# Self attention of a decoder layer: a low score product over 128 rows, and one buffer of normalised outputs

## Chip, cores and metric

The kernel runs on one core of one Trainium2 chip. The metric is the device time of one execution in microseconds, as the median of several. The engines are named as in the profile: PE (TensorE matmuls) with PEld (its weight loads), DVE (VectorE), ACT (ScalarE), POOL (GpSimd) and SP (the DMA queue of SyncE).

## The reference, cut to what matters

One decoder layer over x of 8 batches x 512 tokens x 512 channels, in three blocks: a self attention, a cross attention with a router, and a feed-forward block over routed tokens. Only the first is touched. With h the normalised input, 16 heads of 64 and a causal window of 512 it computes

```
q, k, v = h @ w_q, h @ w_k, h @ w_v            # per head: [512, 64]
ll      = q @ k.T * 64**-0.5, causal
scores  = h @ scorer_w + scorer_b              # the 128 best tokens of the batch ...
attn    = softmax(concat(ll, lg))              # ... count a second time as keys
x       = x + (x' + (attn @ v) @ w_out)
```

A batch is one window of 512 tokens, so that the chosen 128 keys are keys of the window once more; the kernel gives them the weight two ("twice") instead of gathering them.

## The kernel before

`self_attention` runs a prologue (constants, weights split into a high and a low part, the first batch normalised) and then a loop over 8 batches. All four engines walk through one list of steps, `attention_plan()`, in the same order, each doing its part of a step; semaphores tie them together.

**Steps of one batch.** First the value projections (`v`) and the first `q` and `k`. Then 8 pairs of heads (p) with 5 score units each (u), 40 units in all, numbered g = 5p + u. At place g of the list PE does, in this order: the scores of unit g (`s`), the transposes of the probabilities of unit g-2 (`t`), the product with the values of unit g-3 (`pv`), at u = 0 the projection `q` and at u = 2 the projection `k` of the next pair, at four places something of the next batch (at g = 18 `score`, the transposes that make a row of the token scores), and last `ot`, the transposes of a finished pair's normalised outputs. The list puts `ot` of pair p at g = 5p + 9, a place with u = 4. After the pairs comes `out`, the product with w_out.

**A score unit.** u = 0 and u = 1 are one block of 128 queries by 512 keys (head 0 and 1). u = 2 and u = 3 are two blocks, of 128 and of 384 keys. u = 4 is two blocks of 256 keys, one of each head. Each block is three matmuls into `s_bank`: "high" (L661, or L659), 128 rows deep, whose stationary operand is `q_both` (a head's q rounded to fp32r in its own 64 rows and its remainder in the other 64) against `k_twice` (the rounded k in both halves); "low" (L664, or L657), 64 rows deep, the rounded q of the head's own rows against `k_lo`, the remainder of k; and the causal mask (L665), bf16. A pair so has 8 low products. At u = 4 the first block has its low product (L657) first, and PE waits (`s_half`) before the second block's.

**The other engines.** At place g DVE takes the row maxima of unit g (L525, L530), copies the transposed probabilities of unit g-2 to `probs_t` (L538, which the `pv` of that unit reads one place later), normalises the outputs of unit g-3 into `o_norm` (L552, L553), and at u = 3 makes `k_lo` of the next pair (L518), for which the scores of the next pair wait. The copy of the score row into `row_s` (L446) is at g = 18, behind `k_lo`. ACT takes the exponentials (L405), four half copies into `k_twice` at u = 3, and copies `ot` out (L413).

**Banks.** `t`, `score`, `ht` and `ot` take the two banks `pt_bank` in turn, in the order of the list; `PT` is that order. Before PE writes one (`pt_empty`) it waits until the use before the last one has been copied out; of a `score` that is the signal `row_copied` of L446.

`o_norm` has two buffers, one for each parity of the pair; DVE waits at u = 0 for the `ot` of the pair before the last.

Of the kernel before, what the change touches and what calls it, by code (L numbers as in the profile page):

```python
# [18 lines left out]
F32 = mybir.dt.float32  # L19
# [9 lines left out]
P = 128  # L29
# [55 lines left out]
def attention_plan():  # L85

    plan = [("v", i) for i in range(2 * TT - 2)] + [("q", 0), ("q_lo", 0), ("k", 0), ("k_lo", 0)]
    plan += [("v", i) for i in range(2 * TT - 2, 2 * TT)]
    for g in range(NU + 7):
        p, u = divmod(g, UNITS)
        if g < NU:
            plan.append(("s", g))
        if 2 <= g < NU + 2:
            plan.append(("t", g - 2))  # L100
        if 3 <= g < NU + 3:
            plan.append(("pv", g - 3))
        if g < NU and p + 1 < NPAIR and u < 4:
            plan.append((("q", "q_lo", "k", "k_lo")[u], p + 1))
        if g == 5:
            plan.append(("stats", 0))
        if g == 14:
            plan.append(("dot", 0))
        if g == 18:
            plan.append(("score", 0))  # L110
        if g in RANK_AT:
            plan.append(("rank", RANK_AT.index(g)))
        if NU <= g < NU + DC:
            plan.append(("ht", g - NU))
        if g >= 9 and (g - 9) % UNITS == 0 and (g - 9) // UNITS < NPAIR - 1:
            plan.append(("ot", (g - 9) // UNITS))
    plan.append(("ot", NPAIR - 1))
    plan += [("out", t) for t in range(TT)]
    return plan
# [7 lines left out]
def self_attention(nc, x, norm_w, w_q, w_k, w_v, w_out, scorer_w, scorer_b, x1):  # L127
# [3 lines left out]
    with ExitStack() as ctx:  # L131
        def sb(name, shape, dt=F32):
            return ctx.enter_context(nc.sbuf_tensor(name, shape, dt))
# [15 lines left out]
        q_both, k_twice = sb("q_both", [P, 2, 2, S], F32R), sb("k_twice", [P, 2, 2, S], F32R)  # L149
        k_lo = sb("k_lo", [P, 2, S], F32R)  # L150
        probs = sb("probs", [P, 2, 512])
        probs_t = sb("probs_t", [P, 2, 512])
        o_rden = sb("o_rden", [P, 2, 2])
        o_norm = sb("o_norm", [P, 2, TT, 2, HD])
        o_t = sb("o_t", [P, NPAIR, S])
# [4 lines left out]
        before = sb("before", [P, S + P * (TT - 1)], I8)  # L160
        row_s = sb("row_s", [P, S])
        junk = sb("junk", [P, S], BF16)
        carrier = sb("carrier", [P, 4])
# [28 lines left out]
        v_ready, v_sum_ready, qk_hi, qk_lo = sem("v_ready"), sem("v_sum_ready"), sem("qk_hi"), sem("qk_lo")  # L192
        s_ready, s_half = sem("s_ready"), sem("s_half")
        max_ready, p_ready = sem("max_ready"), sem("p_ready")
# [53 lines left out]
        def _(sp):  # L248
# [3 lines left out]
            sp.dma_start(sw[:, :], scorer_w.rearrange("d o -> o d").broadcast_to((P, D))).then_inc(small_in, 16)  # L252
            sp.dma_start(row_s[:, :], norm_w.rearrange("(o d) -> o d", o=1).broadcast_to((P, D))).then_inc(small_in, 16)
            sp.dma_start(sbias[:, :], scorer_b.rearrange("(o d) -> o d", o=1).broadcast_to((P, 1))
# [34 lines left out]
        def _(pl):  # L289
# [17 lines left out]
            nc.gpsimd.tensor_copy(ident_b[:, :], ident[:, :]).then_inc(const_made, 1)  # L307
            nc.gpsimd.memset(junk[:, :], 0.0).then_inc(const_made, 1)
            pl.wait_ge(const_made, N_CONST)
# [106 lines left out]
        def _(dv):  # L416
# [15 lines left out]

            def dot(n):

                dv.wait_ge(h_ready, n * TT + TT)
                for t in range(TT):
                    step(nc.vector.tensor_tensor_reduce(junk[:, :], xb[:, t, :], sw[:, :], 1.0, 0.0, ALU.mult,
                                                             ALU.add, score[:, t:t + 1]))
                done.wait(dv)
                nc.vector.tensor_scalar(score[:, :], score[:, :], sbias[:, 0:1], None, ALU.add).then_inc(score_ready, 1)  # L440

            def score_row(b, n):

                slot, ready = pt(b, ("score", 0))
                dv.wait_ge(pt_ready, ready)
                nc.vector.tensor_copy(row_s[:, :], pt_bank[slot][:, :]).then_inc(row_copied, 1)  # L446

            def rank(b, n, t):

                if t == 0:  # L450
                    dv.wait_ge(row_copied, n + 1)
                step(nc.vector.tensor_scalar(junk[:, :], row_s[:, :], score[:, t:t + 1], None, ALU.is_gt, ALU.add,
                                                  accum_out=cnt[:, 0, t:t + 1]))
                y0 = P * (TT - 1 - t)
                step(nc.vector.scalar_tensor_tensor(junk[:, :], row_s[:, :], score[:, t:t + 1],
                                                         before[:, y0:y0 + S], ALU.is_equal, ALU.mult,
                                                         accum_out=cnt[:, 1, t:t + 1]))
                if t == TT - 1:
                    done.wait(dv)
                    step(nc.vector.tensor_tensor(cnt[:, 0, :], cnt[:, 0, :], cnt[:, 1, :], ALU.add))  # L460
                    if b is not None:
                        dv.wait_ge(v_ready, n * (2 * TT))
                    nc.vector.tensor_scalar(twice[:, :], cnt[:, 0, :], TOPK - 0.5, 1.0, ALU.is_lt,
                                            ALU.add).then_inc(twice_ready, 1)
# [20 lines left out]
            dv.wait_ge(small_in, 64)  # L485
            nc.vector.tensor_tensor(sw[:, :], sw[:, :], row_s[:, :], ALU.mult).then_inc(sw_made, 1)
            dv.wait_ge(sw_made, 1)
            split(0)
            split(1)
            for c in range(DC):  # L490
                normed(None, 0, c)
            dot(0)
            split(2)
# [6 lines left out]
            with dv.Fori(0, B) as b, done.loop(b, 2 * TT + 2 * TT + 1 + NU, B):  # L500
                for kind, i in plan:
# [6 lines left out]
                    if kind in ("q_lo", "k_lo"):  # L508
                        slot, _ = pj(b, (kind[0], i))
                        dv.wait_ge(qk_hi, b * (2 * NPAIR) + 2 * i + (1 if kind == "q_lo" else 2))  # L510
                        for h in range(2):
# [5 lines left out]
                            else:  # L517
                                ins = nc.vector.tensor_tensor(k_lo[own, i % 2, :], pj_bank[slot][own, :],  # L518
                                                              k_twice[own, i % 2, h, :].bitcast(F32), ALU.subtract)
# [19 lines left out]
                    if kind == "pv":  # L539
                        p, u = divmod(i, UNITS)  # L540
                        dv.wait_ge(pv_ready, b * NU + i + 1)
                        if u == 0 and p >= 2:
                            dv.wait_ge(pt_ready, pt(b, ("ot", p - 2))[1])
                        n = len(unit_blocks(u))
                        src = o_bank[i % 2][:, 0:n * VW].rearrange("p (n v) -> p n v", n=n)
                        if u < 2:
                            dst = o_norm[:, p % 2, 3:4, u, :]
                        elif u < 4:
                            dst = o_norm[:, p % 2, 0:3:2, u - 2, :]
                        else:  # L550
                            dst = o_norm[:, p % 2, 1, :, :]
                        step(nc.vector.reciprocal(o_rden[:, i % 2, 0:n], src[:, :, HD]))  # L552
# [5 lines left out]
                    if kind == "dot":  # L558
                        dot(b + 1)
                    if kind == "score":  # L560
# [13 lines left out]
        def _(pe):  # L574
# [46 lines left out]
            with pe.Fori(0, B) as b:  # L621
                for kind, i in plan:
# [22 lines left out]
                    if kind == "s":  # L645
# [6 lines left out]
                        for h, t, c0, nk in unit_blocks(u):  # L652
                            queries, rows = slice(P * t, P * t + P), head_rows(h)
                            high = (q_both[:, p % 2, h, queries], k_twice[:, p % 2, h, 0:nk])
                            low = (q_both[rows, p % 2, h, queries], k_lo[rows, p % 2, 0:nk])
                            if u == UNITS - 1 and h == 0:
                                nc.tensor.matmul(s_bank[slot][:, c0:c0 + nk], *low, start=True, stop=False  # L657
                                                 ).then_inc(s_half, 1)
                                nc.tensor.matmul(s_bank[slot][:, c0:c0 + nk], *high, start=False, stop=False)  # L659
                            else:  # L660
                                nc.tensor.matmul(s_bank[slot][:, c0:c0 + nk], *high, start=True, stop=False)  # L661
                                if u == UNITS - 1:
                                    pe.wait_ge(s_half, b * NPAIR + p + 1)
                                nc.tensor.matmul(s_bank[slot][:, c0:c0 + nk], *low, start=False, stop=False)  # L664
                            ins = nc.tensor.matmul(s_bank[slot][:, c0 + nk - P:c0 + nk], ident_b[:, :], causal_b[:, :],  # L665
                                                   start=False, stop=True)
# [25 lines left out]
                    if kind == "ot":  # L692
# [3 lines left out]
                        for t in range(TT):  # L696
                            ins = nc.tensor.transpose(pt_bank[slot][:, P * t:P * t + P],
                                                      o_norm[:, i % 2, t, :, :].rearrange("p h d -> p (h d)"),
                                                      ident[:, :])
# [1062 lines left out]
```

## Time and profile before

| | us |
|---|---|
| median of 3 runs | 2416.09 (2413.26 to 2416.24) |
| span of the profiled execution, first to last instruction | 2414.0 |
| PE busy | 2241.6 (93%) |
| PEld busy | 1682.4 (70%) |
| DVE busy | 1349.6 (56%) |
| ACT busy | 845.5 (35%) |
| POOL busy | 429.2 (18%) |

The profiled execution's own time is its span, 2414.0 us; the median lies 2.1 us above it. The loop over the batches of the self attention lies between about 32 and 1648 us. Matmuls are pipelined and the ends that the profile gives for them are modelled, so that neighbouring matmuls seem to overlap: what a matmul costs is read from its start to the start of the next one. A time of a row has two decimals, so that a difference of two starts is good to 0.01 us.

### The profile page before, as it was taken

The page shows a single profiled execution, that of the slowest core. Times are in us where ns is not written, and L with a number is a line of the kernel's source. Part 1 is how long each engine was busy: PE and PEld are TensorE (multiplying, and loading weights), DVE is VectorE, ACT ScalarE, POOL GpSimd, SP SyncE. Part 2 cuts the span into 40 slices and gives each one's busy share as a digit, 9 for nine tenths or more (in the row PEclk, how much of TensorE's full clock was granted, in tenths as well). Part 3 has the DMA queues.
Part 4 walks back from the last instruction along what each step waited for, and adds up shares of the span by engine and source line. Part 5 has one row for each costly group of instructions (what it writes and reads, how often), then busy time and mean ns, then how long its engine had stood idle before and what let it go on. Part 6 is the DMA issues. An engine that isn't in the chain of part 4 may idle for free. (4 is left out here: it accounts for less than half of the span.)

```text
span 2414.0 us, 35686 instructions
## 1 busy us (share of the span) xinstructions
PE 2241.6 (93%) x12029; PEld 1682.4 (70%) x12029; DVE 1349.6 (56%) x3145; ACT 845.5 (35%) x1541; POOL 429.2 (18%) x669
## 2 busy tenths in 40 slices
PE   3999999999999999999999999996898888878899
PEld 3786777678678677767767767773787888865543
DVE  4574376177257437617725743661787878845500
ACT  3442344144144234314414423441644444413210
POOL 2100000010010000001001000002866666620000
PEclk9999999999999999999999999997988888858999
DMA  5000000100100000010010000002013211141000
GB/s 183 1 1 31 23 1 10 45 1 1 54 1 1 31 23 1 10 45 1 1 54 1 1 28 27 1 10 91 29 56 102 83 55 55 53 152 50 1 0 18
DMA packets 46136, 80.23 MB, mean 33 GB/s; under 512 B 10067, under 2 KB 10067, under 8 KB 45448
## 3 DMA queue, kind: packets, MB, share of 16 engines
q1 hardware_dynamic: 45320, 75.85, 9.3%
q8 instruction: 103, 1.69, 0.3%
q0 software_dynamic: 640, 2.10, 0.2%
q14 instruction: 73, 0.60, 0.1%
HBM read 60.11 MB, written 17.83 MB: 32 GB/s over the span
## 5 line engine op out<-in xcount | busy, mean ns | idle before, releaser
L405 ACT ACTIVATE probs<-s_bank,nmax 128x512 f32<-128x512 f32 (+3 forms) x512 | 249.4, 525 | 421.6 <-DVE nmax L530 294.3
L530 DVE TENSOR_REDUCE nmax<-s_bank 128x1 f32<-128x512 f32 (+2 forms) x384 | 185.3, 510 | 305.7 <-PE s_bank L665 302.0
L688 PE MATMUL o_bank<-vals,probs_t 128*128 128x65 f32 x2560 | 322.2, 269 | 0.0
L688 PEld LDWEIGHTS o_bank<-vals,probs_t 128*128 128x128 f32 x2560 | 311.0, 192 | 1.4 <-DVE probs_t L538 1.4
L712 PE MATMUL pj_bank<-w_o,o_t 128*128 128x512 f32 x512 | 223.5, 597 | 6.0 <-ACT o_t L413 6.0
L538 DVE COPY probs_t<-pt_bank 128x512 f32<-128x512 f32 x320 | 218.0, 681 | 3.6 <-PE pt_bank L673 3.6
L319 POOL TENSOR_TENSOR idle<-ones 128x4 f32<-128x4 f32 x41 | 8.1, 198 | 1065.7 <-DMA probs<-in_x 1063.7
L673 PE MATMUL pt_bank<-ident,probs 128*128 128x128 f32 x1280 | 194.1, 274 | 0.0
L712 PEld LDWEIGHTS pj_bank<-w_o,o_t 128*128 128x128 f32 x512 | 97.2, 191 | 127.6 <-issue 127.6
L664 PE MATMUL s_bank<-k_lo,q_both 64*128 64x512 f32 (+3 forms) x448 | 184.9, 413 | 0.0
L514 DVE SCALAR_TENSOR_TENSOR q_both<-pj_bank,q_both 64x512 fp32r<-64x512 f32 x128 | 88.2, 689 | 141.6 <-ACT q_both L392 138.9
L661 PE MATMUL s_bank<-k_twice,q_both 128*128 128x512 f32 (+3 forms) x448 | 166.9, 373 | 0.0
L383 ACT ACTIVATE vals<-pj_bank,twice 128x512 f32<-128x512 f32 x64 | 43.9, 688 | 341.8 <-PE pj_bank L579 336.5
L1259 PEld LDWEIGHTS x_o_bank<-vx,p_t 77*128 77x128 f32 x1024 | 148.9, 224 | 17.2 <-issue 10.0
L1259 PE MATMUL x_o_bank<-vx,p_t 77*128 77x33 f32 x1024 | 143.8, 300 | 3.9 <-DVE att L1141 3.9
L570 DVE TENSOR_TENSOR probs<-pj_bank,probs 128x512 f32<-128x512 f32 x32 | 22.1, 692 | 213.8 <-PE pj_bank L712 195.3
L664 PEld LDWEIGHTS s_bank<-k_lo,q_both 64*128 64x128 f32 x448 | 81.9, 183 | 85.5 <-issue 72.1
L673 PEld LDWEIGHTS pt_bank<-ident,probs 128*128 128x128 f32 x1280 | 135.7, 141 | 0.0
L577 PE MATMUL pj_bank<-wv_hi,ht_hi 128*128 128x512 f32 x256 | 104.2, 407 | 22.9 <-ACT vals L383 9.9
L1245 PE MATMUL e_bank<-qk_bd,xl_t 128*128 128x308 f32 x256 | 96.9, 510 | 27.7 <-DVE e L1123 27.0
L1022 POOL TENSOR_TENSOR e<-e,fill 128x616 f32<-128x616 f32 x64 | 95.3, 1489 | 127.1 <-DVE fill L1129 126.9
L665 PE MATMUL s_bank<-causal_b,ident_b 128*128 128x128 bf16 x512 | 117.7, 230 | 0.0
(266 smaller groups left out, 4245.5 us busy)
## 6 DMA issues: line engine op xcount, KB each, us to landing
xb<-in_x SPq DMA_DIRECT2D x9, 1024.0 KB, 5.3
xt<-x SPq DMA_DIRECT2D x36, 256.0 KB, 2.8
probs<-in_x SPq DMA_DIRECT2D x32, 256.0 KB, 2.7
x<-probs SPq DMA_DIRECT2D x32, 256.0 KB, 2.0
am<-in_L_ffn_attention_mask SPq DMA_DIRECT2D x8, 1024.0 KB, 5.2
out<-x SPq DMA_DIRECT2D x32, 256.0 KB, 2.1
w_sb<-in_L_ffn_w SPq DMA_DIRECT2D x2, 4096.0 KB, 20.2
o_t<-in_L_attn_w_v SPq DMA_DIRECT2D x2, 1024.0 KB, 9.5
```

The costliest lines, as they stand in the source:

```text
L405: ins = nc.scalar.activation(probs[:, i % 2, c0:c0 + nk], s_bank[i % 2][:, c0:c0 + nk], ACT.Exp, bias=nmax[:, i % 4, n:n + 1])
L530: ins = nc.vector.tensor_reduce(nmax[:, i % 4, n:n + 1], s_bank[i % 2][:, c0:c0 + nk], AX.X, ALU.max, negate=True)
L538: nc.vector.tensor_copy(probs_t[:, i % 2, :], pt_bank[slot][:, :]).then_inc(ts_ready, 1)
L577: nc.tensor.matmul(out, lhs_hi, rhs_hi, start=start, stop=False)
L661: nc.tensor.matmul(s_bank[slot][:, c0:c0 + nk], *high, start=True, stop=False)
L664: nc.tensor.matmul(s_bank[slot][:, c0:c0 + nk], *low, start=False, stop=False)
L665: ins = nc.tensor.matmul(s_bank[slot][:, c0 + nk - P:c0 + nk], ident_b[:, :], causal_b[:, :], start=False, stop=True)
L673: ins = nc.tensor.transpose(pt_bank[slot][:, P * j:P * j + P], probs[:, i % 2, P * j:P * j + P], ident[:, :])
L688: ins = nc.tensor.matmul(o_bank[slot][:, o0:o0 + VW], probs_t[:, i % 2, c0 + P * kt:c0 + P * kt + P], vals[:, kt, 2 * p + h, :], start=(kt ...
L712: ins = nc.tensor.matmul(pj_bank[slot][:, :], o_t[:, c, P * i:P * i + P], w_o[:, c, :], start=(c == 0), stop=(c == NPAIR - 1))
L1245: ins = nc.tensor.matmul(e_bank[:, c, 0:CH * SK], xl_t[:, (i // 2) % 2, P * k:P * k + P], qk_bd[:, n.par, k].rearrange("p h k -> p (h k)") ...
L1259: ins = nc.tensor.matmul(o_bank[:, VX * h:VX * h + VX], p_t[:, i % 2, h // CH, P * (h % CH):P * (h % CH) + P], vx[:, n.par, 2 * CH * (i % ...
```

## The change

- `k_lo` has a buffer for each head, 128 rows deep, in which the other head's 64 rows are zero. The low product is now 128 rows deep, with the same stationary operand as the high one. POOL clears all of `k_lo` once in the prologue, in place of the former memset of `junk`, before the signal for which DVE and PE start.
- At u = 4 the order is high, low, mask as in the other units, and the wait on `s_half` is gone.
- `o_norm` has one buffer. DVE, at u = 0 of pair p, waits for the `ot` transposes of pair p-1, and the list has `ot` of pair p one place earlier, at g = 5p + 8 (u = 3).
- `row_s` and `junk` are gone: in the prologue they are halves of `probs`, in the loop the last two slices of `o_t`; the unused output `junk` of some reductions is so fp32 instead of bf16.

```diff
-        if g >= 9 and (g - 9) % UNITS == 0 and (g - 9) // UNITS < NPAIR - 1:
-            plan.append(("ot", (g - 9) // UNITS))
+        if g >= 8 and (g - 8) % UNITS == 0 and (g - 8) // UNITS < NPAIR - 1:
+            plan.append(("ot", (g - 8) // UNITS))
...
-        k_lo = sb("k_lo", [P, 2, S], F32R)
+        k_lo = sb("k_lo", [P, 2, 2, S], F32R)
...
-        o_norm = sb("o_norm", [P, 2, TT, 2, HD])
+        o_norm = sb("o_norm", [P, TT, 2, HD])
...
-        row_s = sb("row_s", [P, S])
-        junk = sb("junk", [P, S], BF16)
...
-            sp.dma_start(row_s[:, :], norm_w.rearrange("(o d) -> o d", o=1).broadcast_to((P, D))).then_inc(small_in, 16)
+            sp.dma_start(probs[:, 1, :], norm_w.rearrange("(o d) -> o d", o=1).broadcast_to((P, D))).then_inc(small_in, 16)
...
-            nc.gpsimd.memset(junk[:, :], 0.0).then_inc(const_made, 1)
+            nc.gpsimd.memset(k_lo[:, :, :, :].bitcast(F32), 0.0).then_inc(const_made, 1)
...
+            def spare(b):
+
+                return (probs[:, 0, :], probs[:, 1, :]) if b is None else (o_t[:, NPAIR - 1, :], o_t[:, NPAIR - 2, :])
...
-                nc.vector.tensor_copy(row_s[:, :], pt_bank[slot][:, :]).then_inc(row_copied, 1)
+                nc.vector.tensor_copy(spare(b)[1], pt_bank[slot][:, :]).then_inc(row_copied, 1)
...
-                                ins = nc.vector.tensor_tensor(k_lo[own, i % 2, :], pj_bank[slot][own, :],
+                                ins = nc.vector.tensor_tensor(k_lo[own, i % 2, h, :], pj_bank[slot][own, :],
                                                               k_twice[own, i % 2, h, :].bitcast(F32), ALU.subtract)
...
-                        if u == 0 and p >= 2:
-                            dv.wait_ge(pt_ready, pt(b, ("ot", p - 2))[1])
+                        if u == 0 and p >= 1:
+                            dv.wait_ge(pt_ready, pt(b, ("ot", p - 1))[1])
...
-                            queries, rows = slice(P * t, P * t + P), head_rows(h)
-                            high = (q_both[:, p % 2, h, queries], k_twice[:, p % 2, h, 0:nk])
-                            low = (q_both[rows, p % 2, h, queries], k_lo[rows, p % 2, 0:nk])
-                            if u == UNITS - 1 and h == 0:
-                                nc.tensor.matmul(s_bank[slot][:, c0:c0 + nk], *low, start=True, stop=False
-                                                 ).then_inc(s_half, 1)
-                                nc.tensor.matmul(s_bank[slot][:, c0:c0 + nk], *high, start=False, stop=False)
-                            else:
-                                nc.tensor.matmul(s_bank[slot][:, c0:c0 + nk], *high, start=True, stop=False)
-                                if u == UNITS - 1:
-                                    pe.wait_ge(s_half, b * NPAIR + p + 1)
-                                nc.tensor.matmul(s_bank[slot][:, c0:c0 + nk], *low, start=False, stop=False)
+                            queries = slice(P * t, P * t + P)
+                            both = q_both[:, p % 2, h, queries]
+                            nc.tensor.matmul(s_bank[slot][:, c0:c0 + nk], both, k_twice[:, p % 2, h, 0:nk],
+                                             start=True, stop=False)
+                            nc.tensor.matmul(s_bank[slot][:, c0:c0 + nk], both, k_lo[:, p % 2, h, 0:nk],
+                                             start=False, stop=False)
```

## Rows read from the trace of the kernel before

**Rows 1.** Window 74 to 1616 us: busy PE, PEld, DVE, ACT, POOL; granted clock; DMA.
```profile
74.00:1616.00 1542.00, 1516.27 (x8357) 1134.82 (x8355) 848.48 (x2007) 558.70 (x1035) 84.97 (x198) 1.00 0.05 15
```

**Rows 2.** Timeline of PE, one pair's units: start us, us, then the instruction.
```profile
703.82 0.39 PE L579 MATMUL pj_bank<-ht_lo,wk_hi 128*128 128x512 f32 x1
704.04 0.22 PE L661 MATMUL s_bank<-k_twice,q_both 128*128 128x128 f32 x1
704.19 0.32 PE L664 MATMUL s_bank<-k_lo,q_both 64*128 64x128 f32 x1
...
705.27 0.61 PE L673 MATMUL pt_bank<-ident,probs 128*128 128x128 f32 x4
705.72 1.00 PE L688 MATMUL o_bank<-vals,probs_t 128*128 128x65 f32 x8
706.65 0.38 PE L657 MATMUL s_bank<-k_lo,q_both 64*128 64x256 f32 x1
706.96 0.39 PE L659 MATMUL s_bank<-k_twice,q_both 128*128 128x256 f32 x1
707.19 0.23 PE L665 MATMUL s_bank<-causal_b,ident_b 128*128 128x128 bf16 x1
707.23 0.36 PE L661 MATMUL s_bank<-k_twice,q_both 128*128 128x256 f32 x1
707.52 0.38 PE L664 MATMUL s_bank<-k_lo,q_both 64*128 64x256 f32 x1
707.83 0.23 PE L665 MATMUL s_bank<-causal_b,ident_b 128*128 128x128 bf16 x1
707.90 0.61 PE L673 MATMUL pt_bank<-ident,probs 128*128 128x128 f32 x4
708.34 1.00 PE L688 MATMUL o_bank<-vals,probs_t 128*128 128x65 f32 x8
709.18 0.61 PE L697 MATMUL pt_bank<-ident,o_norm 128*128 128x128 f32 x4
709.55 0.48 PE L661 MATMUL s_bank<-k_twice,q_both 128*128 128x512 f32 x1
709.96 0.49 PE L664 MATMUL s_bank<-k_lo,q_both 64*128 64x512 f32 x1
...
710.45 0.61 PE L673 MATMUL pt_bank<-ident,probs 128*128 128x128 f32 x4
710.89 1.00 PE L688 MATMUL o_bank<-vals,probs_t 128*128 128x65 f32 x8
711.70 0.48 PE L577 MATMUL pj_bank<-ht_hi,wq_hi 128*128 128x512 f32 x1
...
714.55 0.39 PE L661 MATMUL s_bank<-k_twice,q_both 128*128 128x512 f32 x1
714.87 0.49 PE L664 MATMUL s_bank<-k_lo,q_both 64*128 64x512 f32 x1
```

**Rows 3.** Line 664, all its weight loads: what their engine sat idle for.
```profile
  issue: 72.1, 312
```

**Rows 4.** Timeline of DVE beside Rows 2.
```profile
706.76 0.17 DVE L552 RECIPROCAL o_rden<-o_bank 128x1 f32<-128x1 f32 x1
...
707.10 1.38 DVE L518 TENSOR_TENSOR k_lo<-pj_bank,k_twice 64x512 fp32r<-64x512 f32 x2
...
709.12 0.68 DVE L538 COPY probs_t<-pt_bank 128x512 f32<-128x512 f32 x1
```

**Rows 5.** Timeline two pairs later, at places 18 and 19 of the list.
```profile
742.56 0.60 PE L613 MATMUL pt_bank<-ident,score 128*128 128x128 f32 x4
...
744.60 0.69 DVE L446 COPY row_s<-pt_bank 128x512 f32<-128x512 f32 x1
```

**Rows 6.** Timeline of the start.
```profile
3.82 0.51 POOL L308 MEMSET junk<- 128x512 bf16 x1
...
6.14 2.47 DVE L426 BATCH_NORM_STATS2 bn<-xb 128x6 f32<-128x512 f32 x4 [1.67 <-DMA xb<-in_x]
```

More of the change, by code:

```diff
@@ L192, in self_attention @@
         v_ready, v_sum_ready, qk_hi, qk_lo = sem("v_ready"), sem("v_sum_ready"), sem("qk_hi"), sem("qk_lo")
-        s_ready, s_half = sem("s_ready"), sem("s_half")
+        s_ready = sem("s_ready")
         max_ready, p_ready = sem("max_ready"), sem("p_ready")
@@ L431, in stats, with dot @@
                 ins.then_inc(stats_ready, 1)
-            def dot(n):
+            def spare(b):
+                return (probs[:, 0, :], probs[:, 1, :]) if b is None else (o_t[:, NPAIR - 1, :], o_t[:, NPAIR - 2, :])
+            def dot(b, n):
+                junk, _ = spare(b)
                 dv.wait_ge(h_ready, n * TT + TT)
                 for t in range(TT):
-                    step(nc.vector.tensor_tensor_reduce(junk[:, :], xb[:, t, :], sw[:, :], 1.0, 0.0, ALU.mult,
+                    step(nc.vector.tensor_tensor_reduce(junk, xb[:, t, :], sw[:, :], 1.0, 0.0, ALU.mult,
                                                              ALU.add, score[:, t:t + 1]))
@@ L445, in score_row @@
                 dv.wait_ge(pt_ready, ready)
-                nc.vector.tensor_copy(row_s[:, :], pt_bank[slot][:, :]).then_inc(row_copied, 1)
+                nc.vector.tensor_copy(spare(b)[1], pt_bank[slot][:, :]).then_inc(row_copied, 1)
             def rank(b, n, t):
+                junk, row = spare(b)
                 if t == 0:
                     dv.wait_ge(row_copied, n + 1)
-                step(nc.vector.tensor_scalar(junk[:, :], row_s[:, :], score[:, t:t + 1], None, ALU.is_gt, ALU.add,
+                step(nc.vector.tensor_scalar(junk, row, score[:, t:t + 1], None, ALU.is_gt, ALU.add,
                                                   accum_out=cnt[:, 0, t:t + 1]))
                 y0 = P * (TT - 1 - t)
-                step(nc.vector.scalar_tensor_tensor(junk[:, :], row_s[:, :], score[:, t:t + 1],
+                step(nc.vector.scalar_tensor_tensor(junk, row, score[:, t:t + 1],
                                                          before[:, y0:y0 + S], ALU.is_equal, ALU.mult,
@@ L485, in _ @@
             dv.wait_ge(small_in, 64)
-            nc.vector.tensor_tensor(sw[:, :], sw[:, :], row_s[:, :], ALU.mult).then_inc(sw_made, 1)
+            nc.vector.tensor_tensor(sw[:, :], sw[:, :], probs[:, 1, :], ALU.mult).then_inc(sw_made, 1)
             dv.wait_ge(sw_made, 1)
@@ L491, in _ @@
                 normed(None, 0, c)
-            dot(0)
+            dot(None, 0)
             split(2)
@@ L546, in _ @@
                         if u < 2:
-                            dst = o_norm[:, p % 2, 3:4, u, :]
+                            dst = o_norm[:, 3:4, u, :]
                         elif u < 4:
-                            dst = o_norm[:, p % 2, 0:3:2, u - 2, :]
+                            dst = o_norm[:, 0:3:2, u - 2, :]
                         else:
-                            dst = o_norm[:, p % 2, 1, :, :]
+                            dst = o_norm[:, 1, :, :]
                         step(nc.vector.reciprocal(o_rden[:, i % 2, 0:n], src[:, :, HD]))
@@ L558, in _ @@
                     if kind == "dot":
-                        dot(b + 1)
+                        dot(b, b + 1)
                     if kind == "score":
@@ L697, in _ @@
                             ins = nc.tensor.transpose(pt_bank[slot][:, P * t:P * t + P],
-                                                      o_norm[:, i % 2, t, :, :].rearrange("p h d -> p (h d)"),
+                                                      o_norm[:, t, :, :].rearrange("p h d -> p (h d)"),
                                                       ident[:, :])
```

## Prediction

> **What bounds the kernel now.** I read the windows first, to find which engine is full where the change acts. In the pair stage PE is busy for 1516 of 1542 us at a granted clock of 1.00, the full 2.4 GHz, while DVE works 848 and ACT 559 us [rows 1]. Only batch boundaries leave gaps; in a pair PE goes from one instruction to the next. So in this stage the time is what PE needs between two starts, and I read those in the timeline of PE [rows 2]. Then I asked what the weight loads of the low product wait for: nothing, but 312 of the 448 loads of line 664 have idle time before them, 72.1 us together, put down to issue [rows 3]. No other engine's signal ends it. Last come the timelines of DVE at u = 3 and at places 18 and 19, because there the change adds a wait and moves `ot` [rows 4, 5], and the start [rows 6].
>
> **What a 64-row product costs.** Three differences of starts, all at the full clock [rows 2]:
> - Into it. A 512-column product followed by another of 128 rows takes 0.22 to 0.23 us (703.82 to 704.04). The high product followed by the 64-row low one takes 0.32 (714.55 to 714.87). Difference 0.09.
> - Out of it, into the mask. After a 128-row product of 256 columns the mask starts 0.23 later (706.96 to 707.19), after a 64-row one of 256 columns 0.31 (707.52 to 707.83). Difference 0.08; with the rounding I take 0.085.
> - Between units. `pv` to the next start is 0.81 where a 128-row product of the projection follows (710.89 to 711.70) and 0.93 where L657 does (705.72 to 706.65): 0.12.
>
> The 64-row product streams as many columns as the 128-row one, so its depth itself saves nothing. The change makes every product of a block 128 rows deep, so I take both differences away. The one limit is the weight load: in `t`, four products of 128 columns take 0.44 (707.90 to 708.34), 0.11 for each, so that a 128-column product can't be followed by another after less than 0.11.
>
> **Sum for a pair.**
> - u = 0 and 1, one 512-column block each: 0.09 + 0.085, twice: 0.35.
> - u = 2 and 3: the 128-column block saves 0.15 - 0.11 = 0.04 on the way in (704.04 to 704.19) and 0.085 out; the 384-column block 0.09 and 0.085. Together 0.30, twice: 0.60.
> - u = 4: the first block now begins with the high product, so 0.12 between units is saved. L657 to L659 takes 0.31; high to low of 256 columns will take the 0.41 of 709.55 to 709.96 less 0.09 and less 256 columns at 2.4 GHz (0.107), 0.21: saved 0.10. Its way out was already the fast one. The second block saves 0.09 and 0.085. Together 0.395. That it needs no `s_half` is inside these differences.
>
> That is 1.345 us in a pair, and 64 pairs make 86 us.
>
> **One buffer and the earlier `ot`, in an ordinary pair.** PE does the same transposes one place earlier, which costs it nothing. DVE, at u = 0's outputs (place u = 3), now waits for them. Take s of u = 3 as zero. `t` comes at 1.23 - 0.30 = 0.93, `pv` 0.45 later, `ot` another 0.84 later at 2.22 (708.34 to 709.18), and it ends 0.61 later, 2.83. DVE then starts the reciprocal at about 2.87. In the run before it started at 706.76, 2.72 after s. Behind it are queued `k_lo` (0.34 later, 1.38 long), the maxima of u = 4 and the copy of `probs_t` that ends at 709.80, 1.32 after `k_lo` [rows 4]. So `k_lo` ends at 4.59, the copy at 5.91. PE wants `k_lo` for the next pair at 5.51 - 0.30 - 0.395 = 4.81: hidden by 0.2. It wants the copy for `pv` at 4.81 + 1.34 - 0.175 = 5.97: hidden by 0.06, which a signal's way may just use up. I take zero, and keep up to 0.2 for each of the 56 pairs with a predecessor, 11 us, as the bound above; below zero there is nothing to gain, as PE did not wait there.
>
> **Place 18, once a batch.** Here the score row's transposes come between `pv` and the moved `ot`. Before, `ot` of pair 2 was at place 19, behind `t` of unit 17; the bank order was t16, score, t17, ot. Now it is t16, score, ot, t17, so that t17 gets the bank of the score row and must wait for `row_copied`. On DVE that copy stands behind `k_lo`, and `k_lo` behind the new wait for `ot`. With s of unit 18 as zero: score at 2.22, `ot` at 2.66 (four transposes are 0.44), ended at 3.27, DVE's reciprocal 3.31, `k_lo` at 3.65. `k_lo` and the row's copy took 1.38 and 0.69 [rows 5], with some 0.03 between: the copy ends at 5.75. PE would have started t17 at 2.66 + 0.37 (709.18 to 709.55) + 0.98 (the new u = 4: 0.21 + 0.23 + 0.04 + 0.20 + 0.23 + 0.07) = 4.01. It stands still for 1.74 us, 14 us in 8 batches. `k_lo` has long been made when it goes on, so nothing adds to it. The bound below is zero, if another user than the score should precede t17 on its bank; the bound above is 17, with 0.4 for signals and the maxima that queue up.
>
> **The rest.** POOL's memset grows from 512 to 2048 columns. At 0.51 for 512 it would end at 3.82 + 4 x 0.51 = 5.86 at most, and DVE had nothing before x landed at 6.14 [rows 6]: hidden, and if the cover were gone it would move the whole start by its lateness; up to 2 us if 4-byte elements should cost double. fp32 in place of bf16 for an output that nobody reads, and `row_s` in `o_t`, lie on DVE, which has 45% of this stage free [rows 1]: zero, at most 2 us by the four dot products of a batch. DMAs are not moved.
>
> **Sum.** 2414.0 - 86 + 14 = 2342 us of span; the median stands 2.1 above it: 2344.
>
> **Rivals.**
> - *No stall at place 18* (something else frees the bank, or DVE is earlier): 2416 - 86 = 2330. For it, PE never waited there before; against it, the order of the list.
> - *DVE becomes late in every pair*: `k_lo` or the copy misses PE by up to 0.2, or the stages with extra DVE work (statistics, dot products, ranks) queue: 11 us back, 2355. For it, the cover of 0.06; against it, DVE's share.
> - *Only the way in is saved*: the mask's bf16 load may wait for the low product whatever its depth. Then 448 x 0.085 = 38 us stay: 2382. The row 706.96 speaks against it.
> - *Slower: the weight load of the low product is no longer pulled ahead.* A load of 64 rows covers half of the rows (64*128 in the rows), and a full one (128*128) may have to wait until the high product has streamed. The place is each of the 512 low products. A load of 128 columns is worth 0.11 alone and four of them queue at that pace; if it stood bare with another drain of 0.09 behind the product, each would cost 0.20 in place of the 0.09 of today: +56 us, while the ways out give 38 back and place 18 takes 14: 2416 + 32 = 2448. It decides from about 0.05 more for each low product. Against it: the projections are 128 rows deep throughout, and follow each other in 0.22 to 0.23, which is 512 columns at 2.4 GHz (0.213) and next to nothing.
>
> The Trainium skill (TensorE: Matmul & The Clock Gate, "Part 3: Packing small matmuls") says of this that a weight load overlaps running matmuls only when the row group differs. By that the last rival would hold, at 2448. The projections' rows bear this out in no place, and the same page names a background weight buffer as a second way, so I give it little.
>
> **Chances.** Forecast 0.68; no stall 0.12; DVE late 0.12; only the way in 0.04; slower 0.03; something that leaves it within 0.2% 0.01. About 0.2%, 5 us, is what a measurement of this kernel can tell from no change. The first three hold 0.92 and reach from 2330 to 2355; with 2 us for the start on the one side and for rounding (0.01 in each of eight differences, 5 us in all) on both, the range is 2326 to 2360.
>
> **What would show it.** In the changed timeline: high to low of 512 columns 0.23 after a projection and low to mask about 0.34 (0.42 less 0.085); a pair of 16.65 us in place of 18.00; no idle time by issue before the low product's weight loads; PE waiting some 1.7 us for the score row's copy at t17, 8 times; `k_lo` ending 0.2 before the next pair. The prediction is wrong if the starts around the low product stay as they were, or if PE waits for DVE in each pair.

## The result: faster than forecast, 2320 in place of 2344 us

| | before | changed |
|---|---|---|
| median | 2415.06 us (2413.26 to 2416.24, 4 runs) | 2320.44 us (2315.39 to 2326.16, 4 runs) |
| span of the profiled execution | 2414.0 | 2319.7 |
| its own time | 2416.1 | 2321.4 |

The ratio is 0.9604, with a 95% interval of 0.9588 to 0.962. The forecast had the sign, but its gain of 72 us was 22 too small and the range began at 2326. The gain lies in the stage that was changed: the last product with w_out begins at 1653.9 us before and at 1553.6 after, 100.3 earlier. The unchanged rest of the program took 760 and 766 us; in the traces of the experiments it took 755 to 763, so that a difference of a few us between two times need not come from the self attention.

The busy times on the page of the changed kernel:

```profile
PE 2134.8 (92%) x12029; PEld 1665.7 (72%) x12029; DVE 1345.7 (58%) x3145; ACT 844.9 (36%) x1541; POOL 431.3 (19%) x669
```

PE is busy for 107 us less with the same number of instructions, DVE and ACT almost as long as before. Two windows of the changed kernel's trace, behind the last product with w_out and the pair stage before it (busy PE, PEld, DVE, ACT, POOL, then granted clock, DMA share and GB/s):

```profile
1554.00:2320.00 766.00, 664.83 (x3402) 509.05 (x3401) 460.46 (x1063) 258.50 (x474) 325.00 (x428) 0.83 0.17 57
74.00:1554.00 1480.00, 1434.40 (x8495) 1128.59 (x8493) 852.46 (x2026) 562.95 (x1043) 89.19 (x206) 1.00 0.05 17
```

In the pair stage the mean clock is 1.00, as before [rows 1], but PE, which was busy for 98% of it, is now busy for 97%: there are new waits. The timeline of PE in the changed kernel, for the units u = 3, u = 4 and the next pair's u = 0 that [rows 2] shows of before:

```profile
715.76 0.22 PE L659 MATMUL s_bank<-k_twice,q_both 128*128 128x128 f32 x1
715.82 0.28 PE L661 MATMUL s_bank<-k_lo,q_both 128*128 128x128 f32 x1
715.94 0.23 PE L663 MATMUL s_bank<-causal_b,ident_b 128*128 128x128 bf16 x1
...
717.76 0.61 PE L695 MATMUL pt_bank<-ident,o_norm 128*128 128x128 f32 x4
718.12 0.36 PE L659 MATMUL s_bank<-k_twice,q_both 128*128 128x256 f32 x1
718.32 0.28 PE L661 MATMUL s_bank<-k_lo,q_both 128*128 128x256 f32 x1
718.45 0.23 PE L663 MATMUL s_bank<-causal_b,ident_b 128*128 128x128 bf16 x1
...
719.32 1.00 PE L686 MATMUL o_bank<-vals,probs_t 128*128 128x65 f32 x8
720.58 0.49 PE L659 MATMUL s_bank<-k_twice,q_both 128*128 128x512 f32 x1 [0.26 <-DVE k_lo L522]
720.91 0.40 PE L661 MATMUL s_bank<-k_lo,q_both 128*128 128x512 f32 x1
721.15 0.23 PE L663 MATMUL s_bank<-causal_b,ident_b 128*128 128x128 bf16 x1
```

Read the way out of a low product: 256 columns, 718.32 to 718.45, 0.13; 512 columns, 720.91 to 721.15, 0.24. The prediction had 0.23 and 0.34. Each is 0.1 shorter. Read then the bracket of 720.58: here PE waits for `k_lo`, which it never did before in a pair. The DVE lines beside it:

```profile
718.41 0.17 DVE L556 RECIPROCAL o_rden<-o_bank 128x1 f32<-128x1 f32 x1 [0.38 <-PE pt_bank L695]
...
719.06 1.39 DVE L522 TENSOR_TENSOR k_lo<-pj_bank,k_twice 64x512 fp32r<-64x512 f32 x2 [0.23 <-issue]
```

DVE's reciprocal starts when `ot` ends (717.76 + 0.61 = 718.37), and `k_lo` ends at 720.45, 4.69 after s of u = 3 (forecast 4.59). Of the boundaries between two pairs in a batch this one is the worst: `k_lo` starts 0.3 later than elsewhere, behind an idle 0.23 us of DVE that the profile puts down to no other engine. The next boundary, 16.18 later, is an ordinary one. Its s of u = 3 is at 732.27:

```profile
735.25 1.38 DVE L522 TENSOR_TENSOR k_lo<-pj_bank,k_twice 64x512 fp32r<-64x512 f32 x2
737.27 0.68 DVE L542 COPY probs_t<-pt_bank 128x512 f32<-128x512 f32 x1
```
```profile
735.83 1.00 PE L686 MATMUL o_bank<-vals,probs_t 128*128 128x65 f32 x8
736.76 0.49 PE L659 MATMUL s_bank<-k_twice,q_both 128*128 128x512 f32 x1
...
737.40 0.61 PE L671 MATMUL pt_bank<-ident,probs 128*128 128x128 f32 x4
738.01 1.10 PE L686 MATMUL o_bank<-vals,probs_t 128*128 128x65 f32 x8
738.92 0.48 PE L581 MATMUL pj_bank<-ht_hi,wq_hi 128*128 128x512 f32 x1
```
```profile
738.01 0.97 PEld L686 LDWEIGHTS o_bank<-vals,probs_t 128*128 128x128 f32 x8 [0.24 <-DVE probs_t L542]
```

There `k_lo` ends at 736.63, 4.36 after s, and the copy at 737.95, 5.68 after s: each 0.23 earlier than forecast. PE was there first all the same. From `pv` to the next score product are 0.93 us in place of 0.81, from `t` to `pv` 0.61 in place of 0.44, and behind this `pv`, whose weight load could not be made ahead, 0.91 in place of 0.81. And place 18, the timeline one pair before 720.58, with the row of the waits by total behind it (waiting engine, what it waited for, us in all, times, longest):

```profile
700.86 1.38 DVE L522 TENSOR_TENSOR k_lo<-pj_bank,k_twice 64x512 fp32r<-64x512 f32 x2
...
702.27 0.69 DVE L449 COPY o_t<-pt_bank 128x512 f32<-128x512 f32 x1
...
703.11 0.63 PE L671 MATMUL pt_bank<-ident,probs 128*128 128x128 f32 x4 [1.96 <-DVE o_t L449]
```
```profile
PE pt_bank L671 <- DVE o_t L449: 15.7, 8, 2.0
```

That is the stall foreseen for place 18: 8 times 1.96 us idle, where 1.74 was forecast. By starts it is 2.12: t17 would have come 0.07 behind the mask of 700.92.

### The profile page after: what moved, and what is told of

Same layout as the page of the kernel before. It is cut to its first block and busy times, and to the rows that moved or that the text cites. A ratio compares the mean times of both kernels' runs of the same rounds, so it can differ in the third digit from the quotient of the medians.

```text
span 2319.7 us, 35694 instructions
## 1 busy us (share of the span) xinstructions
PE 2134.8 (92%) x12029; PEld 1665.7 (72%) x12029; DVE 1345.7 (58%) x3145; ACT 844.9 (36%) x1541; POOL 431.3 (19%) x669
## 5 line engine op out<-in xcount | busy, mean ns | idle before, releaser
L686 PE MATMUL o_bank<-vals,probs_t 128*128 128x65 f32 x2560 | 329.1, 272 | 0.1
L659 PE MATMUL s_bank<-k_twice,q_both 128*128 128x512 f32 (+3 forms) x512 | 190.1, 373 | 2.1 <-DVE k_lo L522 2.1
L661 PE MATMUL s_bank<-k_lo,q_both 128*128 128x512 f32 (+3 forms) x512 | 164.4, 321 | 0.0
L1243 PE MATMUL e_bank<-qk_bd,xl_t 128*128 128x308 f32 x256 | 101.9, 532 | 26.1 <-DVE e L1121 25.4
L390 ACT ACTIVATE q_both<-pj_bank 64x512 fp32r<-64x512 f32 x128 | 75.7, 592 | 94.0 <-PE pj_bank L583 93.2
```

The lines of the kernel that those rows point to most:

```text
L659: nc.tensor.matmul(s_bank[slot][:, c0:c0 + nk], both, k_twice[:, p % 2, h, 0:nk], start=True, stop=False)
L661: nc.tensor.matmul(s_bank[slot][:, c0:c0 + nk], both, k_lo[:, p % 2, h, 0:nk], start=False, stop=False)
L686: ins = nc.tensor.matmul(o_bank[slot][:, o0:o0 + VW], probs_t[:, i % 2, c0 + P * kt:c0 + P * kt + P], vals[:, kt, 2 * p + h, :], start=(kt ...
L1243: ins = nc.tensor.matmul(e_bank[:, c, 0:CH * SK], xl_t[:, (i // 2) % 2, P * k:P * k + P], qk_bd[:, n.par, k].rearrange("p h k -> p (h k)") ...
```

## The experiments

The kernel before ran beside each on the same chip, and each ratio is to it. Lengths of a pair are from the first score product (512 columns, u = 0) of one pair to that of the next.

**1. The low product without the buffer's wait** (`depth_alone`).

```diff
-        if g >= 8 and (g - 8) % UNITS == 0 and (g - 8) // UNITS < NPAIR - 1:
-            plan.append(("ot", (g - 8) // UNITS))
+        if g >= 9 and (g - 9) % UNITS == 0 and (g - 9) // UNITS < NPAIR - 1:
+            plan.append(("ot", (g - 9) // UNITS))
...
-        o_norm = sb("o_norm", [P, TT, 2, HD])
+        o_norm = sb("o_norm", [P, TT + 1, 2, HD])
...
-                        if u == 0 and p >= 1:
+                        if u == 2 and p >= 1:
...
-                            dst = o_norm[:, 3:4, u, :]
+                            dst = o_norm[:, 3 + p % 2:4 + p % 2, u, :]
...
-                                                      o_norm[:, t, :, :].rearrange("p h d -> p (h d)"),
+                                                      o_norm[:, t if t < 3 else 3 + i % 2, :, :].rearrange("p h d -> p (h d)"),
```

> The 128-row low product, with the transposes `ot` back at g = 5p + 9 and, for the one slice of o_norm that the next pair writes first (tokens 384 to 511), a second copy, so that DVE has nothing to wait for at u = 0. Theory: each of the 512 low products of 64 rows cost a drain before it, a bare load of its own weights and a drain behind it, 0.28 us in all, and the whole change gives 2.2 us a pair, 142 us in all; what the changed kernel lacks of that (some 42 us of the self attention) is waits on DVE, 16 at place 18 and 26 in the ordinary pairs, all made by the earlier ot and the single buffer. Then a pair takes 15.8 us, PE doesn't wait at place 18, and the time is about 2320 - 40 = 2280. Rival: DVE is late in the ordinary pairs by itself, since PE is faster: then only the 16 us of place 18 come back, 2305.

Measured: 2302.38 us (ratio 0.9537, 0.9507 to 0.9567). The stall at place 18 is down to 0.3 us, but an ordinary pair took 16.23, as long as in the changed kernel (16.18). The waits by total name a new one:

```profile
PE pt_bank L671 <- DVE probs_t L542: 11.8, 40, 0.3
```

With `ot` at u = 4 the bank order is t(u2), ot, t(u3), so that t(u3) needs the bank from which DVE copies t(u2), and that copy still stands behind `k_lo`. The rival's time came, though this run doesn't show its reason: one wait had been put in the place of another. Experiment 9 takes the wait away without moving `ot`.

**2. The buffer without the low product** (`buffer_alone`): the kernel before with these lines of the change.

```diff
-        if g >= 9 and (g - 9) % UNITS == 0 and (g - 9) // UNITS < NPAIR - 1:
-            plan.append(("ot", (g - 9) // UNITS))
+        if g >= 8 and (g - 8) % UNITS == 0 and (g - 8) // UNITS < NPAIR - 1:
+            plan.append(("ot", (g - 8) // UNITS))
...
-        o_norm = sb("o_norm", [P, 2, TT, 2, HD])
+        o_norm = sb("o_norm", [P, TT, 2, HD])
...
-                        if u == 0 and p >= 2:
-                            dv.wait_ge(pt_ready, pt(b, ("ot", p - 2))[1])
+                        if u == 0 and p >= 1:
+                            dv.wait_ge(pt_ready, pt(b, ("ot", p - 1))[1])
...
```

> The kernel before with the single o_norm buffer and ot at g = 5p + 8, the low product still 64 rows deep. Theory: PE, slower in every unit, hides DVE's wait in the ordinary pairs (a pair stays at 18.0 us); at place 18 t17 waits for the score row's copy for 2.52 + 0.44 + 0.61 + 0.04 + 0.34 + 2.10 - (2.96 + 0.37 + 1.13) = 1.6 us, 8 times: 2415 + 13 = 2428. Rival: DVE's wait costs in every pair at any speed of PE: over 2440.

Measured: 2446.24 us, ratio 1.0123 (1.0081 to 1.0165): slower by 32 us, not 13. The ordinary pairs are not the reason: they took 18.05, 0.05 more than before. The stall at place 18 is there, and the windows of the stretch behind it show what else happens (columns as above; the last but two is the granted clock):

```profile
762.00:764.00 2.00, 2.00 (x8) 1.12 (x8) 0.83 (x3) 0.00 (x0) 0.00 (x0) 0.50 0.03 8
764.00:768.00 4.00, 4.00 (x15) 3.54 (x14) 1.41 (x4) 0.69 (x1) 0.00 (x0) 0.50 0.00 0
768.00:772.00 4.00, 4.00 (x25) 3.07 (x23) 1.37 (x3) 1.75 (x3) 0.00 (x0) 1.00 0.00 0
```
```profile
758.70 0.23 PE L665 MATMUL s_bank<-causal_b,ident_b 128*128 128x128 bf16 x1
760.21 0.63 PE L673 MATMUL pt_bank<-ident,probs 128*128 128x128 f32 x4 [1.29 <-DVE row_s L446]
...
766.32 0.63 PE L578 MATMUL pj_bank<-ht_hi,wq_lo 128*128 128x512 f32 x1
766.75 0.63 PE L579 MATMUL pj_bank<-ht_lo,wq_hi 128*128 128x512 f32 x1
```

PE stands still for 1.29 us, and then the clock is at 0.50 (1.2 GHz) for some 6 us: products of 512 columns follow each other in 0.43, not 0.23. The unit behind place 19 took 7.5 to 8.5 us in six of the eight batches and its usual 5.0 in two. The last product with w_out came 36.7 us later than in the kernel before (1690.6 and 1653.9). By the lengths of the pairs, 12 us of that are the eight stalls and 18 the six slow units; the rest is the 0.05 us of an ordinary pair and three batches in which the clock fell already before place 20. The theory had the stall, not its price.

**3. The same, with the score row one place earlier** (`buffer_score`).

```diff
-        if g == 18:
+        if g == 17:
             plan.append(("score", 0))
```

> The kernel before with the single buffer and the earlier ot, and the score row at place 17. Theory: the 32 us that the buffer cost in the kernel before were the wait at place 18 (1.3 to 1.6 us, 8 times) and the clock, which fell to 0.50 for some 6 us behind it in most batches (3 us each): without that wait both are gone and the time is that of the kernel before, 2415. Rival: the DVE wait itself costs in the ordinary pairs: 2425 or more.

Measured: 2415.0 us, ratio 0.9988 (0.9964 to 1.0012), the time of the kernel before. An ordinary pair of it, 18.05:

```profile
710.54 0.48 PE L661 MATMUL s_bank<-k_twice,q_both 128*128 128x512 f32 x1
728.59 0.48 PE L661 MATMUL s_bank<-k_twice,q_both 128*128 128x512 f32 x1
```

One place in the list made the whole 32 us. The single buffer is nearly free in the kernel before: 0.05 us a pair, 3 us in all at most, which the total can't tell from nothing. Place 18 with the clock behind it is the rest.

**4. The changed kernel with the score row at place 17** (`score_at_17`): the edit of experiment 3.

> The changed kernel with the score row's transposes and copy one place earlier in the list, at g = 17 (u = 2, where DVE has no k_lo), so that the copy is long done when t17 wants the bank. Theory: the 15.7 us that PE waited for that copy go, less what the k_lo and probs_t waits of that unit take back (0.4 us a batch): 2320 - 12 = 2308. Rival: the wait was only the place where DVE's backlog showed, and it moves to the next unit: no change.

Measured: 2300.2 us (0.9519, 0.9493 to 0.9545), 20 less than the changed kernel. In the traces the last product with w_out comes only 13.0 earlier (1553.6 and 1540.6); the other 8 lie in the unchanged rest (766 and 758) and show nothing of this edit. PE doesn't wait at place 18 any more, but the rival holds in part: the unit behind place 19 takes 5.0 us in each batch, with a wait for the copy of `probs_t` in it, where the changed kernel took 4.70. In two of its eight batches the changed kernel took 6.33 there, at a lower clock (again the last number but two):

```profile
514.00:516.00 2.00, 2.00 (x15) 1.57 (x14) 1.34 (x4) 0.84 (x2) 0.00 (x0) 0.75 0.04 8
516.00:518.00 2.00, 2.00 (x12) 2.00 (x10) 1.13 (x2) 0.69 (x1) 0.00 (x0) 0.50 0.00 0
```

An ordinary pair still takes 16.18:

```profile
714.70 0.49 PE L659 MATMUL s_bank<-k_twice,q_both 128*128 128x512 f32 x1 [0.25 <-DVE k_lo L522]
730.88 0.49 PE L659 MATMUL s_bank<-k_twice,q_both 128*128 128x512 f32 x1
```

**5. Split k_lo as well** (`split_and_score`): experiment 4 with these lines and, not shown, the same split for the first pair and the semaphore `k_first`.

```diff
-        if g < NU and p + 1 < NPAIR and u < 4:
-            plan.append((("q", "q_lo", "k", "k_lo")[u], p + 1))
+        if g < NU and p + 1 < NPAIR:
+            plan.append((("q", "q_lo", "k", "k_lo", "k_lo2")[u], p + 1))
...
-                        ins.then_inc(qk_lo, 1)
+                            if kind == "k_lo":
+                                break
+                        ins.then_inc(qk_lo if kind == "q_lo" else k_first, 1)
+                    if kind == "k_lo2":
+                        slot, _ = pj(b, ("k", i))
+                        own = head_rows(1)
+                        nc.vector.tensor_tensor(k_lo[own, i % 2, 1, :], pj_bank[slot][own, :],
+                                                k_twice[own, i % 2, 1, :].bitcast(F32), ALU.subtract).then_inc(qk_lo, 1)
...
                         if u == 0:
-                            pe.wait_ge(qk_lo, b * (2 * NPAIR) + 2 * p + 2)
+                            pe.wait_ge(k_first, b * NPAIR + p + 1)
+                        if u == 1:
+                            pe.wait_ge(qk_lo, b * (2 * NPAIR) + 2 * p + 2)
...
```

> As score_at_17, and the k_lo of head 1 is made one place later (u = 4), with a signal of its own for head 0, which is all that the first unit of the next pair needs. DVE's queue at u = 3 is 0.69 us shorter. Theory: the waits of the ordinary pairs come from k_lo standing behind DVE's wait for ot and in front of the maxima and the copy of probs_t; they go for the most part: 2308 - 20 = 2288. Rival: the copy of probs_t, which now has the second half in front of it at u = 4, is as late as before: 2308.

Measured: 2279.4 us (0.9428, 0.9402 to 0.9455). An ordinary pair takes 15.74 to 15.78, and PE waits for nobody in it:

```profile
719.45 0.48 PE L668 MATMUL s_bank<-k_twice,q_both 128*128 128x512 f32 x1
...
720.07 0.61 PE L680 MATMUL pt_bank<-ident,probs 128*128 128x128 f32 x4
...
735.19 0.48 PE L668 MATMUL s_bank<-k_twice,q_both 128*128 128x512 f32 x1
```

**6. The price of a 64-row product** (`half_rows_u01`): experiment 5 with

```diff
+                            rows = head_rows(h) if u < 2 else slice(0, P)
-                            nc.tensor.matmul(s_bank[slot][:, c0:c0 + nk], both, k_lo[:, p % 2, h, 0:nk],
-                                             start=False, stop=False)
+                            nc.tensor.matmul(s_bank[slot][:, c0:c0 + nk], q_both[rows, p % 2, h, queries],
+                                             k_lo[rows, p % 2, h, 0:nk], start=False, stop=False)
```

> The kernel with the split k_lo and the score row at place 17, whose ordinary pairs take 15.75 us with no wait, but with 64-row low products again at u = 0 and u = 1 (128 of the 512, all of 512 columns). It prices a 64-row product by itself. Theory (drain, bare load of its own weights 0.11, drain): 0.28 us each, a pair 16.32, in all 36 us: 2279 + 36 = 2315. Rival, the price of the prediction (0.09 in and 0.085 out): 0.175 each, a pair 16.10, 22 us: 2301.

Measured: 2307.36 us (0.9544, 0.949 to 0.9598), between the two. The ordinary pair decides: 16.33, against 16.32 for the theory and 16.10 for the rival. The product stands between 717.38 and 717.81:

```profile
700.65 0.47 PE L668 MATMUL s_bank<-k_twice,q_both 128*128 128x512 f32 x1
...
716.97 0.48 PE L668 MATMUL s_bank<-k_twice,q_both 128*128 128x512 f32 x1
717.38 0.50 PE L671 MATMUL s_bank<-k_lo,q_both 64*128 64x512 f32 x1
717.81 0.23 PE L673 MATMUL s_bank<-causal_b,ident_b 128*128 128x128 bf16 x1
```

In the pair with the score row nothing was lost (16.81 to 16.82), since PE waits there for DVE anyway, behind the dot products (experiment 8); so the total, 28 us, is less than 128 times the price.

**7. Another stationary operand between high and low** (`mask_between`): experiment 5 with the order high, mask, low in each block.

> As that kernel with all low products 128 rows deep, but the order of a block is high, mask, low, so that the two products with the same stationary operand no longer follow each other. Theory: a weight load hides behind what streams before it, the same or not; only where less than 0.11 us streams (the mask's 128 columns, 0.05) some of it shows, up to 0.06 for each low product, 512 of them: at most 31 us, 2279 to 2310, a pair up to 16.2. Rival: high and low follow each other closely because the second load of the same operand is free; then each low product pays a whole load of 0.11: 56 us, 2335, a pair 16.6.

Measured: 2288.77 us (0.9457, 0.9404 to 0.951), a pair of 16.01 (692.88 to 708.91 gives 16.03): 0.25 more for 8 products, 0.03 each, inside the theory's bound and far from the rival's 0.11. It shows in every unit, and more in a block of 512 columns (692.88 to 693.56 is 0.68, in experiment 5 0.62, 719.45 to 720.07) than in a block of 128 (704.44 to 704.68 is 0.24, there 0.21):

```profile
692.88 0.48 PE L668 MATMUL s_bank<-k_twice,q_both 128*128 128x512 f32 x1
693.20 0.23 PE L670 MATMUL s_bank<-causal_b,ident_b 128*128 128x128 bf16 x1
693.24 0.48 PE L672 MATMUL s_bank<-k_lo,q_both 128*128 128x512 f32 x1
693.56 0.60 PE L680 MATMUL pt_bank<-ident,probs 128*128 128x128 f32 x4
...
704.44 0.22 PE L668 MATMUL s_bank<-k_twice,q_both 128*128 128x128 f32 x1
...
704.68 0.39 PE L668 MATMUL s_bank<-k_twice,q_both 128*128 128x384 f32 x1
```

So the gain is not that of a second load of the same operand.

**8. The dot products beside a projection** (`dot_at_10`): experiment 5 with `if g == 14` for ("dot", 0) made `if g == 10`.

> The kernel with the split k_lo and the score row at place 17, and the four dot products of the next batch (3.2 us of DVE) at g = 10 (u = 0, beside a projection) in place of g = 14. Theory: the one wait that is left inside a batch (unit g = 16 takes 2.38 instead of 1.78 us) goes, 0.6 us in each of 8 batches: 2279 - 5 = 2274. Rival: DVE can't hide 3.2 us at u = 0 either, and the wait moves: 2279.

Measured: 2273.19 us, ratio 0.9397 (0.9345 to 0.9449), the fastest of the study. Unit 16 takes 1.78 like the others.

**9. Two copies of one slice, `ot` where the change has it** (`two_slices`): score_at_17 with the o_norm lines of experiment 1, `ot` left at g = 5p + 8.

> As score_at_17 (score row at place 17, ot at g = 5p + 8, k_lo in one step), but with a second copy of the one slice of o_norm that u = 0 and u = 1 write, so that DVE at u = 0 has no ot to wait for; the order of everything is that of score_at_17. Theory: the 0.43 us that an ordinary pair of score_at_17 (16.18) loses against 15.75 come from DVE's wait for ot in front of k_lo; k_lo then ends some 0.7 us earlier and a pair takes 15.75: 2300 - 21 = 2279, as with the split k_lo. Rival: k_lo is late because of ACT's four half copies into k_twice and PE's speed, whatever DVE waits for (the kernel depth_alone took 16.23 a pair without that wait): 2300.

Measured: 2278.94 us (0.9433, 0.9416 to 0.9449), an ordinary pair of 15.75 to 15.80:

```profile
720.40 0.48 PE L659 MATMUL s_bank<-k_twice,q_both 128*128 128x512 f32 x1
736.19 0.48 PE L659 MATMUL s_bank<-k_twice,q_both 128*128 128x512 f32 x1
```

The theory holds: 0.4 us a pair came from DVE's wait for `ot`. The rival that the first experiment had seemed to bear out falls.

## Why the prediction was wrong

**What bounds the kernel** held: PE in the pair stage, and its starts are where the gain is.

**"What a 64-row product costs" is the step that failed**, and in it the way out. The prediction took 0.31 less 0.23, with L659 (706.96 to 707.19 in [rows 2]) as the 128-row product whose way out costs nothing extra. But L659 stood itself behind a 64-row product, so that its own weight load was bare: the 0.23 are a load of 0.11, 256 columns (0.107) and 0.01. The weight loads show it, the first two in the kernel before, the third in the changed one:

```profile
706.96 0.19 PEld L659 LDWEIGHTS s_bank<-k_twice,q_both 128*128 128x128 f32 x1
...
709.96 0.18 PEld L664 LDWEIGHTS s_bank<-k_lo,q_both 64*128 64x128 f32 x1 [0.25 <-issue]
```
```profile
718.21 0.19 PEld L661 LDWEIGHTS s_bank<-k_lo,q_both 128*128 128x128 f32 x1
```

The loads at 706.96 and 709.96 have the same start as their products, the one at 718.21 is 0.11 ahead of its product (718.32), and from there to the mask are 0.13 (718.32 to 718.45). The price of a low product was not 0.09 + 0.085 but a drain of 0.09 on the way in, a bare load of 0.11 and a drain of 0.085 on the way out, 0.28; experiment 6 put it at (16.33 - 15.75) / 2 = 0.29. "Drain" is a name here for time between two products in which nothing in the profile shows. In u = 4 the same 0.11 was missed at L659. That is 0.11 for each of 512 products, 56 us: the term of 86 us was in truth (18.00 - 15.75) x 64 = 144. That the three parts are drain, load and drain is read from starts, of the loads too; only their sum was measured by itself.

**The limit of 0.11 for products of 128 columns** did not show between the starts of high and low, 0.06 apart at 715.76; but low to mask takes 0.12 there, where 128 columns are 0.053. High and low together take 0.18, not the 0.29 that the sum had for them (0.11, and 0.26 less 0.085).

**"One buffer and the earlier ot"** was the second step to fail: DVE's work behind the wait took as long as forecast, the cover was not there. With PE 0.44 faster in u = 3 and u = 4 together than the sum had it, `k_lo` was wanted at 4.37 and not 4.81 after s; in an ordinary pair it ended at 4.36, and the score product came 0.12 late. For the copy the prediction also left out that `probs_t` is what `pv` loads as weights, and that this load starts before the product (710.78 and 710.89 in the kernel before), so that the cover of 0.06 was none even by its own sum. This cost more, 0.17 before `pv` and 0.10 behind it. Together an ordinary pair lost 16.18 - 15.75 = 0.43, in some 6 pairs of a batch, 21 us. This was the rival "DVE becomes late in every pair" at twice its price (11 us, chance 0.12), and it held beside the forecast's mechanism. Experiments 5 and 9, which shorten DVE's queue in two ways, both give it back.

**Place 18** held: 8 x 2.12 = 17 us by starts for 14, the difference being PE's earlier arrival. What no step had is the clock: it fell behind the stall in two of the eight batches of the profiled execution, some 1.6 us each.

The sum with the measured terms is -144 + 17 + 21 + 3 = -103, against 100.3 in the trace. Nearly all that is left is the boundary of 720.58, 0.3 us more than an ordinary one in each batch; why DVE comes late there stays open. The time came out below the range because the missed 58 us of PE's gain were larger than the 27 us of waits and clock that were missed too. As the prediction adds it up, its range would be 2325 to 2362 rather than 2326 to 2360; the measured 2320 lies outside of both.

**The rivals.** "Only the way in is saved" and "slower" fell with the rows at 718.32 and 715.76. The latter was drawn from what the Trainium skill says (TensorE: Matmul & The Clock Gate, "Part 3: Packing small matmuls"), that a load overlaps matmuls only when the row group differs. No row here bears that out: full loads overlap full products throughout (the load at 718.21 beside the product of 718.12; projections of 512 columns 0.22 to 0.23 apart), and it was the change of depth that kept them apart. That fits another page of the Trainium skill (TensorEngine Tiling (Array Packing), "Key Properties"): changing the tiling mode drains the engine. It gives no figure; here it was 0.28 to 0.29 us for one 64-row product between full ones, its bare load included.

**POOL's memset, fp32 outputs, the moved row**: the sum above leaves them a few us together at most; they were not tried by themselves.

## What to carry to other kernels

In this kernel a product over half of the rows between products over all of them saved no time and cost a drain on each side and a weight load that nothing hid, 0.28 to 0.29 us in all; zeros in the unused rows were cheaper. When a difference of two rows is taken as a price, look at what stands before the reference row too, for it can carry part of the price itself. And when PE gets faster than planned, count the covers of the other engines again: of 144 us that PE gained, some 40 went into waits that had been hidden or were new, and moving two steps in the list and splitting a third brought them back (2320 to 2273 us, of which 42 lie in the self attention, 1553.6 to 1512.0).

## What was not expected of the hardware

A wait of 1.3 us in a stage where PE is otherwise always busy was followed by some 6 us at 1.2 GHz, in six of the eight batches of `buffer_alone`, and so cost some 3 us more than itself. The 2.0 us waits of the changed kernel were followed by a slower unit in two of eight only, 1.6 us each. Why a longer wait does so less often stays open.
